# Attention scores on two row halves of the TensorE array, reduced and exponentiated two banks at a time

## The reference

```
qh = layernorm(x) @ Wq.T    # 32 heads of 16
kh, vh = ctx @ Wk.T, ctx @ Wv.T    # 8 groups of 16, each for 4 heads
score = einsum('bhqd,bhkd->bhqk', qh, kh) / sqrt(16)
attn = softmax(score); out = einsum('bhqk,bhkd->bhqd', attn, vh)
x = x + tanh(g_xattn) * (out @ Wfc.T + bfc)
shared = (silu(h @ G.T) * (h @ U.T)) @ Dn.T    # h = layernorm(x)
routed = the same with a second set of weights, times the softmax weights of the top two of 8 logits
x = x + tanh(g_ffn) * (shared + routed)
```

## Time and profile before

| | us |
|---|---|
| timed runs, median of 3 | 955.55 |
| lowest, highest | 951.3, 956.73 |
| profiled execution, its own time | 942.72 |
| its span, first to last instruction | 940.9 |
| PE busy in the span | 899.5 (96%) |
| DVE, ACT, POOL busy | 646.6, 343.4, 486.7 |
| mean granted TensorE clock | 0.987 of full |

### The profile page before, as it was taken

The page is one execution under the profiler, slowest core; times in us unless marked ns, Lnnn a source line. Parts: engine busy times, 40 slices in busy tenths (PEclk is TensorE's granted clock), DMA queues, the critical chain, the costliest instruction groups (busy, mean ns, idle before and its releaser), DMA issues.

```text
span 940.9 us, 14873 instructions
## 1 busy us (share of the span) xinstructions
PE 899.5 (96%) x4896; PEld 697.8 (74%) x4896; DVE 646.6 (69%) x1083; ACT 343.4 (37%) x637; POOL 486.7 (52%) x485
## 2 busy tenths in 40 slices
PE   4689999999999999999999999999999999999998
PEld 3556766676677665688888888887688888888887
DVE  6678888778878887566656566567766656566566
ACT  5165566556655686212212122136212211122112
POOL 4201201300130299878766696663778766696650
PEclk9789999999999999999999999999999999999999
DMA  8863344435343420211111121111312111121102
GB/s 277 201 144 80 78 116 74 108 80 118 62 96 83 87 37 25 90 45 67 45 60 52 45 67 45 45 57 56 112 45 68 45 54 57 45 67 45 45 1 89
DMA packets 42346, 70.83 MB, mean 75 GB/s; under 512 B 5312, under 2 KB 21184, under 8 KB 42048
## 3 DMA queue, kind: packets, MB, share of 16 engines
q1 hardware_dynamic: 42304, 70.29, 27.9%
HBM read 55.33 MB, written 14.68 MB: 74 GB/s over the span
## 4 chain that ended last, share of the span: by engine, by line
PE 72%; issue 17%; DVE 4%; DMA 3%; POOL 2%; ACT 2%; SPq 0%; POOLq 0%; DVEq 0%; ACTq 0%
PE bank L1241 21%; PE bank L1243 20%; PE bank L1242 20%; PE bank L1316 3%; PE bank L1296 3%; PE bank L1306 3%; PE bank L1246 1%; POOL xa L461 1%; DMA q_scr<-qx_l 1%; POOL cx_l L430 1%; DVE mcol L887 1%; PE bank L1565 1%; DVE x_l L1206 1%; DMA wfc_raw<-wfc 1%; DMA xa<-x 1%
## 5 line engine op out<-in xcount | busy, mean ns | idle before, releaser
L887 DVE TENSOR_REDUCE mcol<-bank 128x2 f32<-128x512 f32 x256 | 169.8, 677 | 48.9 <-PE bank L1296 48.1
L1241 PE MATMUL bank<-x_l,w_h 128*128 128x512 f32 x504 | 197.5, 392 | 2.7 <-DVE u L1077 2.5
L1243 PE MATMUL bank<-x_h,w_h 128*128 128x512 f32 x504 | 196.4, 390 | 0.0
L1242 PE MATMUL bank<-x_h,w_l 128*128 128x512 f32 x504 | 196.4, 390 | 0.0
L740 ACT ACTIVATE probs<-bank 128x512 f32<-128x512 f32 x256 | 150.1, 594 | 120.6 <-PE bank L1306 119.5
L595 ACT ACTIVATE hT_h<-bank 128x512 fp32r<-128x512 f32 x72 | 43.2, 599 | 360.3 <-DVE bank L1179 351.5
L551 POOL TENSOR_TENSOR w_l<-raw,w_h 128x512 fp32r<-128x512 f32 (+1 forms) x144 | 162.1, 1159 | 2.9
L1089 DVE SCALAR_TENSOR_TENSOR xa<-bank,tgf,xa 128x512 f32<-128x512 f32 x128 | 96.1, 751 | 77.7 <-PE bank L1243 77.6
L1296 PE MATMUL bank<-k_st,q_st 65*128 65x256 f32 x512 | 114.0, 312 | 11.8 <-DMA q_st<-q_scr 7.1
L1296 PEld LDWEIGHTS bank<-k_st,q_st 65*128 65x128 f32 x512 | 92.9, 201 | 43.1 <-DVE mcol L887 16.6
L430 POOL TENSOR_TENSOR cx_l<-cx_raw,cx_h 128x512 fp32r<-128x512 f32 x12 | 15.5, 1295 | 191.4 <-ACT cx_h L595 191.4
(11 more groups left out here) (148 smaller groups left out, 1362.8 us busy)
## 6 DMA issues: line engine op xcount, KB each, us to landing
raw<-w_gu SPq DMA_DIRECT2D x36, 512.0 KB, 3.3
q_st<-q_scr SPq DMA_DIRECT2D x96, 128.0 KB, 3.8
dnraw<-w_dn SPq DMA_DIRECT2D x36, 256.0 KB, 2.6
xa<-x SPq DMA_DIRECT2D x4, 1024.0 KB, 7.6
cx_raw<-ctxT SPq DMA_DIRECT2D x16, 256.0 KB, 3.4
q_scr<-qx_h SPq DMA_DIRECT2D x16, 256.0 KB, 2.1
q_scr<-qx_l SPq DMA_DIRECT2D x16, 256.0 KB, 2.2
out<-xa SPq DMA_DIRECT2D x16, 256.0 KB, 2.0
```

The source lines that it names most:

```text
L887: v.tensor_reduce(mcol[:, par, at:at + 2], bank[u % sm_banks(n)][:, :].rearrange("p (r k) -> p r k", r=2), AX.X, ALU.max).then_inc(max_ok, 1)
L1241: mm(out, a_h, b_l, start=start, stop=False, skip_group_check=onto)
L1242: mm(out, a_l, b_h, start=False, stop=False, skip_group_check=onto)
L1243: return mm(out, a_h, b_h, start=False, stop=stop, skip_group_check=onto)
```

## The change

Scores: `q_st` and `k_st` now hold the stack twice, on rows 0-63 and on rows 64-127. The first and second half of a chunk's channels go to the two halves, so each half holds 4 of the 8 heads (the weight columns of Wq are reordered on the host so that each half has two heads of each group), and both hold all of k. The stack is 48 deep, with the maximum 49. `sm_pair` issues four 256-column matmuls, alternating between the two row halves of the array (64 rows by 128 columns each) into two banks; `st_pair` issues two of 512 columns. A step has 4 pairs `v` instead of 8 units.

Maxima and exponentials: the banks 0-1 and 2-3 are now two tensors of two banks (`two0`, `two1`). `maximum` reduces both banks of a pair in one instruction, and one ACT instruction exponentiates both. A pair of maxima needs both banks of `two0`, and the next pair is written into the same banks; the same holds for `two1`.

DMAs: `read_q` and `read_k` issue 6 DMAs instead of 3. `read_q` waits for the previous step's value product (`scored(n)`, `pv_ok`) where it waited for the last `st_unit`. The writes of Q are moved to the start of the steps 5, 6, 7 and 0, ahead of `read_q` and `put_max`; `load_cx` moves ahead of `put_max`.

Filler: it stands behind the strips of `pv_unit` in the pair, and its places in the block are new; so are the places of the small ACT and DVE jobs. `aT` has two buffers, `w_h0` and `w_l0` have memory of their own outside attention's, and a memset of `q_st` is gone.

```diff
-SM = P // 2 + 1
+SM = 3 * DH
 MROW = SM
 ST = MROW + 1
+ROWS = P // 2
...
             def read_q(tb, bb, c, n, fresh):
                 if not fresh:
-                    sp.wait_ge(st_full, UNITS * n)
+                    scored(n)
                 sp.wait_ge(q_wr[c], 32 * (tb + 1))
-                for row, part in ((0, 0), (DH, 0), (2 * DH, 1)):
-                    src = q_scr[part, tb, c, :, bb * S:(bb + 1) * S].rearrange("(h d) q -> d h q", d=DH)
-                    sp.dma_start(r(q_st[row:row + DH, c, :, :]), src).then_inc(q_rd[c], 16)
+                for e in range(2):
+                    for row, part in ((0, 0), (DH, 0), (2 * DH, 1)):
+                        src = q_scr[part, tb, c, e * ROWS:(e + 1) * ROWS,
+                                    bb * S:(bb + 1) * S].rearrange("(h d) q -> d h q", d=DH)
+                        at = e * ROWS + row
+                        sp.dma_start(r(q_st[at:at + DH, c, :, :]), src).then_inc(q_rd[c], 16)
...
-                        nc.scalar.activation(probs[:, p, 2 * (u % 2):2 * (u % 2) + 2, :],
-                                             STB[u % 2][:, :].rearrange("p (r q) -> p r q", r=2),
-                                             ACT.Exp, scale=float(DH) ** -0.5).then_inc(exp_ok, 1)
+                        nc.scalar.activation(probs[:, p, :, :], two[1][:, :, :].rearrange("p e (r q) -> p (e r) q", r=2),
+                                             ACT.Exp, scale=float(DH) ** -0.5).then_inc(exp_ok, 2)
...
-                v.tensor_reduce(mcol[:, par, at:at + 2], bank[u % sm_banks(n)][:, :].rearrange("p (r k) -> p r k", r=2),
-                                AX.X, ALU.max).then_inc(max_ok, 1)
+                at = mcol[:, par, :].rearrange("p (e g j t) -> p e g j t", e=2, g=2, t=2)[:, :, g2, :, qt]
+                v_in = two[v % (sm_banks(n) // 2)][:, :, :].rearrange("p e (r k) -> p e r k", r=2)
+                nc.vector.tensor_reduce(at, v_in, AX.X, ALU.max).then_inc(max_ok, 2)
...
-            def sm_unit(n, u, bb, c):
+            def sm_pair(n, v, bb, c):
+
+                qt, g2 = v % 2, v // 2
                 banks = sm_banks(n)
-                if not (isinstance(n, int) and n == 0 and u < banks):
-                    pe.wait_ge(max_ok, UNITS * n + u + 1 - banks)
+                if not (isinstance(n, int) and n == 0 and 2 * v < banks):
+                    pe.wait_ge(max_ok, UNITS * n + 2 * v + 2 - banks)
                 for j in range(2):
-                    h = g2 * RH + half * 2 + j
-                    last = mm(bank[u % banks][:, j * S:(j + 1) * S], q_st[0:SM, c, h, qt * P:(qt + 1) * P],
-                              k_st[0:SM, bb, 2 * c + g2, :], start=True, stop=True)
-                last.then_inc(sm_full, 1)
+                    for e in range(2):
+                        rows = slice(e * ROWS, e * ROWS + SM)
+                        last = mm(bank[(2 * v + e) % banks][:, j * S:(j + 1) * S],
+                                  q_st[rows, c, 2 * g2 + j, qt * P:(qt + 1) * P],
+                                  k_st[rows, bb, 2 * c + g2, :], start=True, stop=True)
+                        if j == 1:
+                            last.then_inc(sm_full[e], 1)
...
+            def st_pair(n, v, bb, c):
+
+                kt, g2 = v % 2, v // 2
+                if not (isinstance(n, int) and n == 0 and v == 0):
+                    pe.wait_ge(exp_ok, UNITS * n + 2 * v)
+                for e in range(2):
+                    rows = slice(e * ROWS, e * ROWS + ST)
+                    mm(STB[e][:, :], k_st[rows, bb, 2 * c + g2, kt * P:(kt + 1) * P],
+                       q_st[rows, c, 2 * g2:2 * g2 + 2, :], start=True, stop=True).then_inc(st_full[e], 1)
```

More of the change, by code:

```diff
@@ L146, in build @@
         raw, w_h, w_l = (raw0, raw1), (w_h0, w_h1), (w_l0, w_l1)
-        bank = [ctx.enter_context(nc.psum_tensor(f"bank{i}", [P, 512], f32)) for i in range(8)]
+        two = [ctx.enter_context(nc.psum_tensor(f"two{i}", [P, 2, 512], f32)) for i in range(2)]
+        bank = [two[i // 2][:, i % 2, :] for i in range(4)]
+        bank += [ctx.enter_context(nc.psum_tensor(f"bank{i}", [P, 512], f32)) for i in range(4, 8)]
         STB, OTB, TPB, PJ = bank[2:4], bank[4], bank[5], bank[6:8]
@@ L338, in body @@
                     n = STEPS * t + s
-                    if s + 3 < STEPS or not last and s != 6:
+                    if s == 0 and not first:
+                        write_q_high(t, 3)
+                        write_q_low(t, 3)
+                    if not last and s >= 5:
+                        write_q_high(t + 1, s - 5)
+                        write_q_low(t + 1, s - 5)
+                    if s + 3 < STEPS or not last:
                         e = s + 3
@@ L342, in body @@
                         read_q(tb, e % STEPS // CHUNKS, e % CHUNKS, n, first and s == 0)
-                    if not last:
-                        if s == 4:
-                            write_k(t + 1)
-                        if s == 6:
-                            write_q_low(t + 1, 1)
-                            read_q(t + 1, 0, 1, n, False)
+                    if s in (0, 2) and not last:
+                        load_cx(t + 1, s)
+                        load_cx(t + 1, s + 1)
+                    if s == 4 and not last:
+                        write_k(t + 1)
                     if not last or s + 1 < STEPS:
@@ L443, in _ @@
             pool.wait_ge(order, 2)
-            g.memset(q_st[0:SM, :, :, :].bitcast(f32), 0.0).then_inc(consts, 1)
             def deviations(lot):
@@ L968, in _ @@
             q_low(0, 2)
-            for u in range(UNITS):
-                maximum(0, u, 0)
-            for u in range(UNITS):
-                maximum(1, u, 1)
+            for k in range(UNITS // 2):
+                maximum(0, k, 0)
+            for k in range(UNITS // 2):
+                maximum(1, k, 1)
             wfc_low()
@@ L1349, in _ @@
             pe.wait_ge(consts, CONSTS)
[L1350 to L1353 removed]
+            pe.wait_ge(k_rd[0], 96)
+            pe.wait_ge(q_rd[0], 96)
+            for v in range(UNITS // 2):
+                sm_pair(0, v, 0, 0)
             mt_job(0, 0)
@@ L1356, in _ @@
             vt_job(0, 0)
-            pe.wait_ge(q_rd[1], 48)
-            for u in range(UNITS):
-                sm_unit(1, u, 0, 1)
+            pe.wait_ge(q_rd[1], 96)
+            for v in range(UNITS // 2):
+                sm_pair(1, v, 0, 1)
             q_job(3, q_lo, 2)
@@ L1476, in body @@
-                        if s == 7 and u == 5 and not last:
-                            pe.wait_ge(q_lo, CHUNKS * nx + 3)
+                        if not first:
+                            if s == 0 and v == 0:
+                                pe.wait_ge(vt_cp, 2 * t + 1)
+                                f_part(t - 1, 1, 0, 0)
+                            if s == 0 and v in (1, 2):
+                                f_part(t - 1, 1, 0, v)
+                            if s == 1 and v == 0:
+                                f_part(t - 1, 1, 0, 3)
+                            if s == 1 and v == 2:
+                                pe.wait_ge(f_add, TILES * t - 1)
+                            if s == 1 and v >= 2:
+                                f_part(t - 1, 1, 1, 2 * v - 4)
+                                f_part(t - 1, 1, 1, 2 * v - 3)
@@ new lines, in body @@
+                        if s == 2 and v == 2:
+                            pe.wait_ge(vt_cp, 2 * t + 2)
+                            if not first:
+                                pe.wait_ge(f_add, TILES * t)
+                        if s == 2 and v >= 2 or s == 3 and v in (1, 2):
+                            kv_part(nx, 0, v - 2 if s == 2 else v + 1)
+                            kv_part(nx, 1, v - 2 if s == 2 else v + 1)
+                        if s == 3 and v == 3:
+                            pe.wait_ge(v_cp, nx + 1)
+                            q_part(nx, 0, 0)
@@ new lines, in body @@
+                        if s == 6 and v == 0:
+                            q_part(nx, 2, 1)
+                        if s == 6 and v == 1:
+                            q_part(nx, 2, 2)
+                            q_part(nx, 2, 3)
+                        if s == 6 and v == 2:
+                            pe.wait_ge(f_add, TILES * t + 1)
+                            f_part(t, 0, 1, 0)
+                        if s == 6 and v == 3:
+                            for part in range(1, DC):
+                                f_part(t, 0, 1, part)
```

426 lines of the change are left out of this document (215 added, 211 removed).

## The result

| | before | after |
|---|---|---|
| timed runs, median (lowest to highest) | 954.67 us (951.3 to 956.73, 4 runs) | 964.43 us (964.41 to 964.62, 4 runs) |
| profiled execution: time, span, mean clock | 942.7, 940.9, 0.987 | 964.6, 962.8, 0.959 |

The ratio of the timed runs is 1.0128, 95% interval 1.0087 to 1.017: slower by about 1.3%, 23 us above the forecast of 941 and 2.4 us above the upper end of its range, 962. In a later series of 8 runs the same kernel took 960.89 us (951.75 to 968.03), ratio 1.0052 (1.0002 to 1.0101). It is slower in both, by 5 to 10 us; the two traces differ by 21.9 us, because the profiled execution of before, at 942.7 us, was faster than every other timed run of it (945.9 to 965.5).

What follows compares the result with a forecast made beforehand. PE was taken as the bound, DVE next. Middle blocks -10.6 us, start and first block +1.4, last block -5.6 sum to -14.8 us: median 941 us from 955.55, 8-in-10 range 915 to 962.

Steps and rivals of the forecast that it cites:

- Scores: PE, middle blocks: row halves overlap fully, a pair takes 0.47 us instead of 0.94, saving 15.0 us per block.
- B: Rival: weight loads of the two halves go one after the other; slower by 19 us, 974 us; chance 0.14.
- C: Rival: the two row halves do not overlap at all; 996 us; chance 0.05.
- Changes of shape: PE, between scores and filler: 0.20 us per change of array shape, 44 changes, 8.8 us per middle block.
- rival A: A change of the array's shape costs nothing; about 35 us saved, 920 us; chance 0.15.
- SP's term: Added read issues and Q's writes ahead make put_max late; 1 us lost per middle block.
- Rival D: SP is late: put_max takes 4.24 us to land, 5.7 us lost per block; 956 us, no change; chance 0.13.
- In the start: Start and first block: second st_pair 6 us late, other seven steps save 4.6 us, net loss 1.4 us.
- I keep the 5.2 us of holes: PE, middle blocks: holes, 85.9 us less the 80.7 us sum of PE's work, stay unchanged despite tighter coupling.
- Middle blocks without the doubled k: Middle blocks: forecast at about 80.6 us each, saving 5.3 us each, 10.6 us together.
- Maxima and exponentials: DVE and ACT: a paired maximum takes 1.14 us, a paired exponential about 1.1 us; both stay hidden.
- The last block: PE saves 7.0 us there; with POOL the next bound, the feed-forward part starts 5.6 us earlier.

Runs made afterwards that it cites:

- run 2: The kernel before with scores 48 and 49 rows deep on a 64-row tile, nothing side by side: 1003.98 us profiled, no interval.
- run 1: The changed kernel with three k reads instead of six, k in rows 0-63 alone, so half the scores are wrong: 937.76 us, ratio 0.9824.
- run 4: The changed kernel with one group per row half, so each half reads only that group's k: 940.17 us, ratio 0.9831.
- run 10: The kernel of Run 8 with output projection and V's transpose moved into step 2's pairs without filler: 934.27 us, ratio 0.9801.
- run 3: The changed kernel with maxima and exponentials taken by two one-bank instructions per pair: 961.7 us, ratio 1.0112.
- 11: The kernel of run 10 with read_q released by the previous step's last scores: 931.24 us, ratio 0.9763.
- Run 8: The kernel of run 4 with four output projection parts in the last block spread over steps 5 and 6: 939.62 us, ratio 0.9818.
- run 13: The changed kernel with the six k reads issued on ACT's own DMA queue instead of by SP: 951.94 us, ratio 0.9981.
- run 14: The changed kernel measured again, unaltered, on the chip of run 13: 960.89 us (951.75 to 968.03), ratio 1.0052.
- kernel 6: The changed kernel with read_q released by the previous step's last scores instead of its value product: 956.03 us, ratio 1.0033.

## Why the prediction was wrong, step by step

**Scores, right.** A pair takes 0.47 us as forecast, so 15 us per block were saved; rivals B and C fall. **Changes of shape, right.** They cost 0.20 us each, in the changed kernel and in run 2; rival A falls. What the Trainium skill's page "TensorEngine Tiling (Array Packing)" says under "Key Properties", that changing the tiling mode drains the engine and that different tiles can load weights and multiply in parallel, agrees with these rows: 0.32 to 0.34 us at a change instead of 0.235, and the two halves' matmuls starting within 4 ns of each other.

**SP's term failed.** I took 1 us per block. Laid beside run 1, the steps 5 and 6 of the three blocks take 7.0, 6.8 and 5.7 us more, 19.5 where I had 3. The step that failed is "0.9 us to issue, 2.2 us to land" for the writes of Q, with the doubled `read_k` given no price in the middle blocks at all. The writes stand behind six reads of k, of 128 KB each, that land one per 1.1 us, so they landed 6.1 and 7.5 us after their issue, and the data of q were there 14 us into step 5 where I had 9.5. The 3.8 us of the earlier trace rows that I took for the landing of a read of q were not the fault: these reads landed in 2.0 to 2.3 us. In the 11 us from the moment k is ready (197.9) to the moment PE wants q (209.0), the queue has to hold the reads of k (until 206.4), the writes of Q (208.8) and the read of q (213.7). Before, it held three reads of k, and Q's first write was a step earlier. Rival D had the size (5.7 us per block) and the direction, but the wrong place: it blamed `put_max`, whose waits hold only 2.3 us. I had priced the move of Q's writes as two issues and not as a place behind k. In the start it is similar: the second `st_pair` group came at 67.1 us, as forecast, but by another sum. The first was 4.7 us late, where run 1 with three reads less is on time (51.0), and the third came at 80.2 us (run 1: 70.8), where I had the block recovering.

**"I keep the 5.2 us of holes" failed too, unseen in the sum.** Run 1's third block is the cleanest view, at a granted clock of 1.00 like its counterpart before. PE's work in it is 74.25 us, where I had 74.4. But of my 5.2 us only 2.5 were holes; the rest was work that my sum of 80.7 lacks, since PE was busy for 82.7. The holes of run 1 there are 5.65 us: PE's wait for maxima went from 1.9 to 4.9 us per block. What my sum of PE's work lacked before, the tighter coupling of the pairs put back as holes. The sign that I had named, maxima coming to rule the pairs, was there for some of them.

**Middle blocks without the doubled k, near.** They take 83.5 and 79.9 us in run 1 and 85.1 and 81.5 in run 4, mean 82.5, where I had 80.6; with filler moved, run 10 has 81.6 and 79.2. **Maxima and exponentials, right in size:** 1.216 and 1.023 us for 1.14 and 1.1, and by run 3 it does not matter whether one instruction or two take them.

**The clock was missing from the sum.** The hole of 4.9 us was followed by 4 us of work at half clock, which takes 2 us more than at full clock. In the steps 5 and 6 the clocks above give 10, 7 and 7 us at half clock where run 1 has none, and PE's waits for q there are only 2.9, 4.9 and 2.4 of the 19.5 us; most of the rest is the clock: some 20 us of the work there ran at half clock, which is an estimated 10 us more. Over the whole execution the mean clock of 0.959 against 0.976 to 0.98 in runs 1, 4 and 10 is 34 to 42 us more at half clock, by the same formula. As an estimate that costs up to half, 17 to 21 us; it overlaps with the waits above and cannot be added to them.

**The last block failed as well:** 77.4 us instead of 67.0, and 76.1 to 76.7 even in the kernels 4, 10 and 11. I had let PE's work shrink by 7 us and kept its holes. Its busy time fell by 3.4 us (6.2 in run 4, at a clock of 0.98), and its idle time rose from 3.4 to 11.5 (13.1 in run 4). PE's waits there name what for, in the changed kernel and then before:

```profile
PE two L1333 <- DVE mcol L909: 6.9, 10, 1.3
PE two L1346 <- ACT probs L751: 4.0, 6, 1.4
```

```profile
PE bank L1306 <- ACT probs L740: 1.8, 4, 0.5
...
PE bank L1296 <- DVE mcol L887: 0.6, 2, 0.5
```

Some of them in order of time:

```profile
347.34 0.50 PE L1333 MATMUL two<-k_st,q_st 48*128 48x256 f32 x4 [0.65 <-DVE mcol L909]
...
361.00 0.65 PE L1333 MATMUL two<-k_st,q_st 48*128 48x256 f32 x4 [1.32 <-DVE mcol L909]
...
378.12 0.51 PE L1333 MATMUL two<-k_st,q_st 48*128 48x256 f32 x4 [1.00 <-DVE mcol L909]
...
382.18 0.50 PE L1346 MATMUL two<-q_st,k_st 49*128 49x512 f32 x2 [1.37 <-ACT probs L751]
```

Where filler is thin, scores, maximum and the next scores into the same two banks are one chain, and PE being faster does not shorten it. I had written this ("where they are absent a hole stays") and given it no microseconds. That PE waits for maxima and exponentials there is shown; that the pairing of the banks is the reason is a reading of these rows. Run 8 moved filler about and did not shorten the block, and no run gave the pairs a second set of banks, so it is not shown. POOL was not the bound: its first weights are ready at 394.1 us, and PE starts on them at 401.5:

```profile
389.45 4.65 POOL L559 TENSOR_TENSOR w_l<-raw,w_h 128x512 fp32r<-128x512 f32 x4
```

**The sum, again.** With k at its old size the forecast of 941 us is what run 4 measures (940.2), but in part by luck. Against the profile of before, run 4's trace saves 5.2 us in the middle blocks (forecast 10.6), nothing in the start and first block (a loss of 1.4 forecast) and loses 3.5 in the last (5.6 saved in the forecast): 1.8 us in all, where I had 14.8. The timed gain is 15 us because the profiled execution of before, at a clock of 0.987, was 12 us faster than its typical one; taking the saving off the median carried that over. What a typical execution of before loses, and in which block, no trace here shows. Open is also how the changed kernel's loss divides: run 13 gives 9 us to the place of the k reads in the queue, and 12 more separate it from run 4, presumably for their bytes and the start.

## What to carry to other kernels

A transfer that a change doubles has to be followed to what stands behind it in the same queue: write down the window from the moment its data are ready to the moment the next consumer wants its own, and fill it with landing times in a burst, not with issues and a median. Before copying an operand into both halves of the array, look for a split of the work in which each half needs only its own part; here that alone turned a loss of 1% into a gain of 1.7%. Where an engine gets faster by pairing buffers, price the pairs that have no cover as a chain of their own: here PE's wait for maxima grew from 4.5 to 22.8 us. A hole costs more than its length where the clock falls in it.

## What the runs showed of the hardware

Reads of 128 KB from DRAM in rows of 1 KB land one per 1.1 us when queued, with the DMA engines 97% busy and moving 145 GB/s, other transfers included. The reads of 64 KB of kernel 4 land one per 0.48 us, which is the pace at which SP issued them, so they show no limit of the engines. Executions of one kernel scatter with the granted clock: in run 14 one took 951.75 us at a mean clock of 0.978 and another 964.62 at 0.963; the feed-forward part is equally long (561.3 or 561.4 us) in 12 of 16 traces and 1.3 us longer in the others. In one run of kernel 6 a hole of 2.2 us left the clock up, in the changed kernel one of 2.9 us at the same place was followed by 10 us at 1.2 GHz; why executions of the same program differ in this I can't say.
